# Four-layer vision tower on one core: expert up-projection on two row halves, output weights counted apart, and a later sum in the last stage

## What is computed

```
def _L0_ffn_ref(hidden_states, router_w, router_b, w1, w2, w3):
    route = jax.nn.softmax(hidden_states @ router_w + router_b, axis=2)
    max_prob = jnp.max(route, axis=2).reshape(-1, 1)
    max_ind = jnp.argmax(route, axis=2).reshape(-1)
    x = hidden_states.reshape(-1, h)
    for e in range(N_EXPERTS):                     # 8 experts, hidden width 512
        mask = (max_ind == e)[:, None]
        xe = jnp.where(mask, x, 0.0)
        oe = jax.nn.silu(xe @ w1[e]) * (xe @ w2[e]) @ w3[e]
        out = out + jnp.where(mask, oe, 0.0)
    out = out.astype(jnp.bfloat16) * max_prob
...
def _L3_ffn_ref(x, router_w, w1, w2):              # 16 experts, widths 128 and 256, top 8
    probs = jax.nn.softmax(logits, axis=-1)
    topk_w, topk_idx = jax.lax.top_k(probs, TOP_K)
    for e in range(NUM_EXPERTS):
        h = jax.nn.gelu(xt @ w1[:, off:off + wd])
        out = out + comb[:, e:e + 1] * (h @ w2[off:off + wd, :])
...
h = h + _L0_ffn_ref(_layernorm(h, axis=-1), ...)
...
h = h + _L3_ffn_ref(_layernorm(h, axis=-1), L3_ffn_router_w, L3_ffn_w1, L3_ffn_w2)
return h
```

## Time and profile before

| | |
|---|---|
| median of three runs | 675.52 us (673.91 to 679.44) |
| the profiled execution | 674.66 us, of which the profile's span is 672.8 us |
| PE busy | 636.1 us (95%) |
| DVE busy | 418.5 us (62%) |
| ACT busy | 315.1 us (47%) |
| granted TensorE clock, mean | 0.99 of full |
| the sorted stage | about 80 us to 187 us of the span |
| the last stage | about 583 us to the end |

### The profile page before, as it was taken

One profiled execution on the slowest core, in us unless ns is written; L12 is line 12 of the kernel. 1 busy time (PEld: TensorE's weight loads), 2 busy tenths in 40 slices (PEclk: granted clock), 3 DMA queues, 4 the chain that ended last, 5 costly groups with the idle time before them and its releaser, 6 DMA issues.

```text
span 672.8 us, 14722 instructions
## 1 busy us (share of the span) xinstructions
PE 636.1 (95%) x5831; PEld 553.5 (82%) x5831; DVE 418.5 (62%) x1108; ACT 315.1 (47%) x731; POOL 114.1 (17%) x108
## 2 busy tenths in 40 slices
PE   6999989999999999999999999999999999999996
PEld 6789876666968778988899988999999868789985
DVE  2746573454369457886736536786766648457784
ACT  0256303222221346885356524555545367466652
POOL 1200000022020314440120000364424110100000
PEclk9999999999999999998999989999999999999998
DMA  9960001466500001110000101222213002021100
GB/s 267 382 192 3 3 0 63 169 248 233 157 1 1 1 1 50 47 50 2 1 1 7 45 2 40 75 66 65 85 63 82 23 1 58 2 87 56 49 1 27
DMA packets 16643, 45.54 MB, mean 68 GB/s; under 512 B 3580, under 2 KB 4572, under 8 KB 14847
## 3 DMA queue, kind: packets, MB, share of 16 engines
q1 hardware_dynamic: 13704, 37.75, 17.7%
q0 software_dynamic: 896, 5.77, 2.5%
q10 hardware_dynamic: 1976, 1.08, 0.7%
HBM read 44.12 MB, written 0.44 MB: 66 GB/s over the span
## 4 chain that ended last, share of the span: by engine, by line
PE 76%; DVE 12%; ACT 7%; issue 3%; DMA 1%; POOL 1%; DVEq 0%; SPq 0%; ACTq 0%
PE PS L1044 7%; PE PS L816 6%; PE PS L911 6%; PE PS L986 5%; PE PS L920 4%; PE PS L1007 3%; PE PS L674 2%; PE PS L1034 2%; PE PS L839 2%; PE PS L1147 2%; PE PS L678 2%; PE PS L676 2%; PE PS L675 2%; PE PS L677 2%; PE PS L854 2%
## 5 line engine op out<-in xcount | busy, mean ns | idle before, releaser
L2280 POOL TENSOR_TENSOR rstd<-var,nhalf 96x3 f32<-96x3 f32 x18 | 17.3, 960 | 288.6 <-DVE var L1582 288.6
L674 PE MATMUL PS<-XH,WH 128*128 128x288 f32 x156 | 48.0, 308 | 3.4 <-DVE OT L1851 1.4
L1303 ACT ACTIVATE MIX<-PS 128x288 f32<-128x288 f32 x54 | 22.2, 411 | 51.6 <-PE PS L678 51.4
L676 PE MATMUL PS<-XH,WL 128*128 128x288 f32 x156 | 46.0, 295 | 0.0
L677 PE MATMUL PS<-X,WH 128*128 128x288 f32 x156 | 46.0, 295 | 0.0
L675 PE MATMUL PS<-XL,WH 128*128 128x288 f32 x156 | 46.0, 295 | 0.0
L678 PE MATMUL PS<-X,WL 128*128 128x288 f32 x156 | 45.9, 294 | 0.0
L1434 ACT ACTIVATE VS<-PS 128x384 f32<-128x384 f32 x48 | 23.1, 486 | 32.1 <-PE PS L986 25.1
L726 PE MATMUL PS<-AH,DW 128*128 128x288 f32 x102 | 32.4, 318 | 4.4 <-DVE AL L1862 4.2
L2126 DVE TENSOR_REDUCE sm<-PS 72x8 f32<-72x288 f32 (+1 forms) x32 | 14.5, 454 | 33.9 <-PE PS L1007 23.4
L911 PE MATMUL PS<-wqkv_l1f,XT 128*96 128x256 f32 (+1 forms) x144 | 34.3, 387 | 0.8 <-ACT XT L1195 0.8
(11 more groups left out here) (313 smaller groups left out, 1798.1 us busy)
## 6 DMA issues: line engine op xcount, KB each, us to landing
RG<-in_gu_l0f_dram SPq DMA_DIRECT2D x4, 1024.0 KB, 8.6
GU<-in_gu_l0f_dram SPq DMA_DIRECT2D x4, 1024.0 KB, 12.4
RG<-in_gu_l2f_dram SPq DMA_DIRECT2D x9, 384.0 KB, 3.5
RG<-in_gu_l2f_dram SPq DMA_DIRECT2D x18, 192.0 KB, 4.2
RD<-in_wd_l2f_dram SPq DMA_DIRECT2D x9, 288.0 KB, 3.0
RD<-in_wd_l3f_dram SPq DMA_DIRECT2D x6, 384.0 KB, 3.3
BIG<-in_patch_dram SPq DMA_DIRECT2D x6, 288.0 KB, 7.1
RD<-in_wd_l0f_dram SPq DMA_DIRECT2D x4, 384.0 KB, 8.2
```

The costliest lines, as they stand in the source:

```text
L674: mm(o, WH[r][:, 0, w], XH[:, cols], start=True, stop=False)
L676: mm(o, WL[r][:, 0, w], XH[:, cols], start=False, stop=False)
```

## The change

It has three parts.

1. **Up-projection on row halves.** `XNS` has 512 columns: the high part of the last 64 features twice (256:384) and their rest twice (384:512). `gather` has four products instead of three for each group; both last ones add up in chunk 1, so that each row half of `XS[:, 1]` has the full last 64 features. `up(i)` makes chunk 0 as before (2 matmuls of 512 columns), and chunk 1 with 4 matmuls of 256 columns and 64 rows each: rows 0:64 for the gate bank and rows 64:128 for the up bank, in turns. ACT's and DVE's instruction on the last 64 features write 128 columns for a group instead of 64.
2. **Output weights counted apart.** The WD transfers have semaphores of their own (`m0_in_down`, `m0_over_down`). `up(i)` waits for GU alone, `down(i)` for WD. On SP and on POOL the GU transfer of the next tile is issued ahead of the WD transfer of this one.
3. **Half 0 of the last stage.** `by_tokens(0)` stands behind `down(45)` instead of `down(42)` on PE, and DVE's `second_sum(M3, 0)` stands in the unit loop ahead of `weigh(44)` instead of behind all units.

```
-                expert(e)
+                expert_up(e)
+                if e > RING0:
+                    expert_down(e - 1)
+            expert_down(E0 - 1)
...
-                    if u - m.lag == m.half_end(0) + 2:
+                    if u - m.lag == m.half_end(0) + (5 if m is M3 else 2):
                         by_tokens(0)
...
-                        for part, c in ((0, 0), (1, 0), (2, 1)):
+                        for part, c in ((0, 0), (1, 0), (2, 1), (3, 1)):
                             last = mm(PS[:, GATHER[n] + c, 0:HID0], XNS[:, g, 128 * part:128 * (part + 1)], PM[:, n % 2, g, :],
-                                      start=(g == 0 and part != 1), stop=(g == NG - 1 and part != 0), skip_group_check=True)
+                                      start=(g == 0 and part % 2 == 0), stop=(g == NG - 1 and part % 2 == 1), skip_group_check=True)
...
                     if i < E0:
-                        pe.wait_ge(m0_in[i % RING0], 32 * (i // RING0 + 1))
+                        pe.wait_ge(m0_in[i % RING0], 16 * (i // RING0 + 1))
...
                     for k in range(2):
-                        for c in range(2):
-                            last = mm(PS[:, up_bank(i) + k, 0:HID0], XS[:, c, i * S0:(i + 1) * S0], w[:, c, k * HID0:(k + 1) * HID0],
-                                      start=(c == 0), stop=(c == 1))
+                        mm(PS[:, up_bank(i) + k, 0:HID0], XS[:, 0, i * S0:(i + 1) * S0], w[:, 0, k * HID0:(k + 1) * HID0],
+                           start=True, stop=False, skip_group_check=True)
+                    for part in range(2):
+                        for k in range(2):
+                            rows, cols = slice(64 * k, 64 * (k + 1)), slice(part * HID0 // 2, (part + 1) * HID0 // 2)
+                            last = mm(PS[:, up_bank(i) + k, cols], XS[rows, 1, i * S0:(i + 1) * S0],
+                                      w[rows, 1, k * HID0:(k + 1) * HID0][:, cols], start=False, stop=True, skip_group_check=True)
...
                 def down(i):
 
+                    if i < E0:
+                        pe.wait_ge(m0_in_down[i % RING0], 16 * (i // RING0 + 1))
+                    else:
+                        pe.wait_ge(m0_over_down[i - E0], 16)
...
+                    if m is M3 and u - m.lag == m.half_end(0) + 1:
+                        second_sum(m, 0)
                     if not m.up and 0 <= u - m.lag + 3 < m.units:
                         weigh(u - m.lag + 3)
...
-                    V.tensor_tensor(XNS[:, gs, 320:384], XN[:, gs, 128:C], XNS[:, gs, 256:320].bitcast(F32),
+                    V.tensor_tensor(XNS[:, gs, 384:512].rearrange("p g (r f) -> p g r f", r=2),
+                                    XN[:, gs, 128:C].unsqueeze(2).to_broadcast([TP, TAU, 2, 64]),
+                                    XNS[:, gs, 256:384].bitcast(F32).rearrange("p g (r f) -> p g r f", r=2),
                                     ALU.subtract).then_inc(S["m0_xlo"], 1)
...
-                second_sum(M3, j)
+                if j:
+                    second_sum(M3, j)
                 stream(len(STAGES), j)
...
-                        pool.wait_ge(S["m0_down"], E0 - RING0 + n_ + 1)
-                        G.indirect_dma_start(WD[b], None, t["wd_l0f"], at).then_inc(m0_over[n_], 16)
+                        if n_:
+                            spare_down(n_ - 1)
+                    spare_down(T0 - E0 - 1)
```

More of the change, by code:

```diff
@@ L418, in bass_vit_tower @@
         DW.append(sb("DW1", [128, 4, 2 * C], F32R))
-        XNS = over("XNS", [TP, NG, 384])
+        XNS = over("XNS", [TP, NG, 512])
         YS = over("YS", [128, T0, 2 * C])
@@ L447, in bass_vit_tower @@
         m0_over = [sem(f"m0_over{r}") for r in range(T0 - E0)]
+        m0_in_down = [sem(f"m0_in_down{r}") for r in range(RING0)]
+        m0_over_down = [sem(f"m0_over_down{r}") for r in range(T0 - E0)]
         in_w2 = [sem(f"in_w2_{k}") for k in range(3)]
@@ L546, in slots, with expert_up @@
                     down_weights(m, s)
-            def expert(e):
+            def expert_up(e):
                 r = e % RING0
@@ L553, in expert, with expert_down @@
                 sp.dma_start(GU[r], t["gu_l0f"][128 * e:128 * (e + 1), :]).then_inc(m0_in[r], 16)
+            def expert_down(e):
+                r = e % RING0
                 if e >= RING0:
                     sp.wait_ge(S["m0_down"], e - RING0 + 1)
-                sp.dma_start(WD[r], t["wd_l0f"][128 * e:128 * (e + 1), :]).then_inc(m0_in[r], 16)
+                sp.dma_start(WD[r], t["wd_l0f"][128 * e:128 * (e + 1), :]).then_inc(m0_in_down[r], 16)
             qkv(A0)
@@ L560, in _ @@
             for e in range(RING0):
-                expert(e)
+                expert_up(e)
+                expert_down(e)
             for c in range(NC_):
@@ L804, in up @@
                     if i < E0:
[L805 removed]
+                        pe.wait_ge(m0_in[i % RING0], 16 * (i // RING0 + 1))
                     else:
[L807 removed]
+                        pe.wait_ge(m0_over[i - E0], 16)
                     pe.wait_ge(S["m0_xs"], 2 * (i * S0 // HID0 + 1))
@@ L1225, in half @@
                     activation(XNS[:, gs, 0:128], XN[:, gs, 0:128], ACT.Copy).then_inc(S["m0_xhi"], 1)
-                    activation(XNS[:, gs, 256:320], XN[:, gs, 128:C], ACT.Copy).then_inc(S["m0_xhi"], 1)
+                    activation(XNS[:, gs, 256:384].rearrange("p g (r f) -> p g r f", r=2),
+                               XN[:, gs, 128:C].unsqueeze(2).to_broadcast([TP, TAU, 2, 64]), ACT.Copy).then_inc(S["m0_xhi"], 1)
                     act.wait_ge(S["ln_turned"], 2 * k + j + 1)
@@ L2268, in pads, with spare_down @@
                     last.then_inc(S["qk_pads"], 1)
+            def spare_down(n_):
+                b = (E0 + n_) % RING0
+                pool.wait_ge(S["m0_down"], E0 - RING0 + n_ + 1)
+                G.indirect_dma_start(WD[b], None, t["wd_l0f"], bass.IndirectOffsetOnAxis(ap=oidx[:, n_:n_ + 1], axis=0)
+                                     ).then_inc(m0_over_down[n_], 16)
             y = n = 0
```

## The result

Twenty runs of each kernel: the changed kernel takes 671.79 us (median; 666.09 to 684.7), the kernel before 675.47 (670.26 to 679.73). The ratio is 0.9944, with a 95% interval of 0.992 to 0.9968: 0.56% less time, 3.8 us of 675.5. One execution of the changed kernel, the one of 684.7 us, was in a slower state and stays out of the ratio. The gain lies within the 1% that I had called no change, and inside the range. The profiled execution of the changed kernel took 669.4 us with a span of 667.7 at a mean granted clock of 0.991, beside 674.66 and 672.8 at 0.990 before. Profile against profile is 5.3 us. Experiment 5 shows how far two executions of one kernel can differ.

The account below looks back on a forecast made before the run. The prediction took PE's own work to bound the sorted stage and a 2.41 us PE wait the last stage. From the profiled 674.66 us, -0.5 for the sorted stage and -3.7 for the end gave 670.4 us, range 665.5 to 678.

Parts of the forecast that it names:

- Gather, front: Sorted stage: 18 more gather matmuls cost +4.2 us, the doubled DVE instruction on the last 64 features +0.1 us.
- Chunk 1: Half-row part of up in the sorted stage: 1.07 us a tile instead of 1.72, -7.8 us over 12 tiles.
- rival A: Half-row products of up overlap only in order of issue, 5 slots a tile: 670.4 us in total, chance 0.45.
- B: Half-row products of up overlap fully, 0.86 us a tile: sorted stage -3.1 us, total 667.9 us, chance 0.25.
- my two witnesses in the earlier trace: Two forms of the attention product L1034, 0.56 and 0.60 us, read as evidence that row halves overlap.
- The sign of 1.2 to 1.3 us: Expected in the changed profile: time from a tile's first half-row record of up to its transposes in the sorted stage.
- Changes of mode: Sorted stage: going from full to half rows and back costs 0.25 us a tile, +3.0 us over 12 tiles.
- Part 2, price 0: Separate semaphores and new issue order for output weights in the tile loop: cost 0, worst end 1 us.
- Part 3: End of the last stage: moving half 0's work saves 3.7 us, 2.57 wait plus 1.54 slow clock less 0.4.
- Rival D: Last stage doesn't gain, as PE waits elsewhere or the clock falls for another reason: 674.1 us, chance 0.05.
- Rival C: Half-row products of up in the sorted stage don't overlap, stage +7.3 us: total 678.3 us, chance 0.15.
- Rival E: Clock dips, as in an attention stage, go or come elsewhere, 2 to 3 us: 667.5 or 673.3 us, chance 0.10.

Follow-up runs that it names:

- Experiment 5: The changed kernel with three matmuls nobody reads ahead of PE's wait near the end of two attentions: 670.23 us, ratio 0.9945 to the kernel before.
- the run without turns: The changed kernel with one half-row matmul of 512 columns for each row half instead of two of 256 in turns: ratio 0.9921 to the kernel before.
- the run on one half: The changed kernel with all four half-row matmuls of a tile on rows 0:64: ratio 1.0096 to the kernel before.

## Why the prediction was right, and where not

- **The bound.** PE sets the sorted stage, and a wait sets the end: both right. The half-speed clock behind that wait is in the profile, but not in every execution.
- **Gather, front.** +4.2 and +0.1 us: 18 records at 0.23 are 4.1; the front's cost is too small to be read.
- **Chunk 1 (rival A against B).** This term was mis-sized. I chose 5 slots by order of issue, 1.07 us a tile; it is 4 slots, 0.86. Of my two witnesses in the earlier trace rows I followed the one with wider output, 0.60 us, which fitted the model to 0.01 us by way of a guessed 0.1 for a change; the other, at 0.56 us, had already contradicted the model. As an estimate, full overlap of the four parts (8 x 0.030) with the 0.35 of two changes gives 0.59 us, so the row of 0.60 could not tell the two models apart. The run without turns excludes order of issue, so rival B's overlap is the true one. The sign of 1.2 to 1.3 us for the part came out as 1.06. The page "TensorE: Matmul & The Clock Gate" of the Trainium skill, Part 3, has matmuls start in program order, which I had read as order of issue between records of one matmul too; the 1.06 us of the run without turns don't bear out that reading.
- **Changes of mode.** Mis-sized the other way: 0.25 us a round trip taken, 0.20 + 0.15 = 0.35 measured (entry 1.06 - 0.86, exit 0.59 - 0.44), 4.2 us in all where 3.0 stood. The other value in the prediction, a record's tail of 0.16 us for each change and 3.8 us in all, was nearer. The page "TensorEngine Tiling (Array Packing)" of the Trainium skill, section Tiling Modes, says that a change drains TensorE. The trace agrees in kind: each way costs time, 0.20 and 0.15 us. The two errors per tile, -0.21 and +0.10, make the stage -1.9 us where I had -0.5. By the pieces (674.66 - 1.9 - 3.7 = 669.1) the truth lies between A's 670.4 and B's 667.9: B's overlap with a dearer change than either had.
- **Part 2, price 0.** The price is right for this change, the reason given was wrong. I argued from the lead of GU, three turns, and from "it never waited for it visibly". WD has a lead of one turn, and 1.1 us of it were left over. Nor did GU have three turns before the change: SyncE issued that of tile 6 at 129.84, behind a WD, and `up` came for it at 139.78, two turns later. Three turns (126.88 to 140.49) are what the new order gives. A wait that isn't visible isn't one that is far away: without the new semaphores the half rows would have lost 0.44%. The parts are not additive, and I added them. The rate that I had bounded at 310 GB/s is 360 in that window, and no wait for a DMA came of it.
- **Part 3.** -3.7 forecast, -3.7 read in the profile and by the medians of the kernel with it alone. The wait, 2.2 us net, was rightly priced. The 1.54 us of slow clock were counted as certain from one profile, and two of five profiles with the old end don't have them: there the number owes something to luck. The schedule step by step has 4.3 us from the last record of down(42) to that of down(47), and 4.31 came; the 4.7 that stands among the signs did not follow from it. Rival D fell. Whether DVE's early copy was needed was not asked: it brings 0.4 us and takes 0.2.
- **Rival C** fell by the run on one half: without overlap the turn would be 5.52 us and the kernel 1% slower than before. **Rival E** is real: in the changed kernel's profile the 12 records of the earlier trace rows are still slow, if less so (3.66 us where they took 4.09), and those at 316 us are slow (4.43 us) where the kernel before has 2.89. From one execution to the next it is of about the size given. That it is chance alone, and no effect of the change, is not shown: the lower clock in the median (0.986 against 0.990) leaves it open.

The forecast difference was -4.3 us (670.4 against the 674.66 of the profiled execution), the medians give -3.8 and the pieces -5.6, or -4.1 without the slow clock of the old end. That the total came so near owes something to luck: two terms of the sorted stage erred against each other, and what they left over, 1.4 us too little gain, stands against 1.5 us of slow clock that were counted as certain.

## What to carry to other kernels

Splitting half-height fp32 matmuls over both row halves gave the full factor of two here, in both orders and all three cuts that were run, but each tile pays some 0.35 us to go there and back. As an estimate from that, it pays from about 0.7 us of half-height work in a group, and one group is better than two. Before a loop is made shorter, work out for every load it waits for the slack (lead less landing time), not whether there is a wait now; a semaphore that carries two loads has the slack of the later one. And look for a change of 0.5% in the timeline of the place first, since single executions here differ by more. But take the clock of a stretch from several executions before a slow stretch is counted as a gain.

## What the hardware showed that was not expected

- The cut of the columns does not matter to the overlap: 4 records of 512, 8 of 256 and 16 of 128 columns over two halves take 1.06, 1.06 and 1.09 us.
- The clock can fall long after the last idle time. In the kernel with the last stage's part alone PE's last wait, 0.84 us, ended at 225.36 us. It was busy without a gap from there on, and stood at half clock from about 240 to 250 (columns as in the earlier trace rows):

```profile
235.00:240.00 5.00, 5.00 (x31) 3.88 (x30) 0.84 (x2) 1.36 (x3) 2.28 (x1) 1.00 0.00 0
240.00:245.00 5.00, 5.00 (x18) 3.65 (x18) 0.39 (x2) 0.61 (x2) 0.00 (x0) 0.54 0.00 0
245.00:250.00 5.00, 5.00 (x13) 3.40 (x12) 1.47 (x6) 0.17 (x1) 0.00 (x0) 0.50 0.00 0
```

  The kernel with the down weights alone ran the same stretch at 1.00. What sets this off stays open.
- The length of an idle time doesn't tell whether the clock falls behind it. The same wait of 2.41 or 2.40 us in the last stage was followed by half clock in three profiles and by full clock in two; 1.68 us there was followed by full clock in the one profile that has it; 0.52 us in an attention was followed by slow records in eleven profiles of thirteen.
